# Cross-attention loop: half of the low softmax weights on GpSimd, one maximum a slot, key chunks of the pair after next begun early

## What is computed

```python
kv_rope = kv_c * cos + rotate_half(kv_c) * sin                 # 4096 x 128
q_r     = einsum('bshq,hqr->bhsr', q_big, W_qr)                # 16 heads, 256 x 64
k_r     = einsum('bld,hdr->bhlr', kv_rope, W_kr)               # 16 heads, 4096 x 64
scores  = einsum('bhsr,bhlr->bhsl', q_r, k_r)
attn    = softmax(scores, axis=-1)
ctx_c   = einsum('bhsl,bld->bhsd', attn, kv_rope)              # 16 heads, 256 x 128
```

## Time and profile before

| | us |
|---|---|
| median of 3 runs | 735.45 (735.08 to 735.92) |
| profiled execution | 732.78 |
| its span | 731.0 |
| loop over the pairs, first score to last low part | 84.25 to 501.44 |

### The profile page before, as it was taken

One profiled execution on the slowest core, in us unless ns is written; L12 is line 12 of the kernel. 1 busy time (PEld: TensorE's weight loads), 2 busy tenths in 40 slices (PEclk: granted clock), 3 DMA queues, 4 the chain that ended last, 5 costly groups with the idle time before them and its releaser, 6 DMA issues.

```text
span 731.0 us, 14846 instructions
## 1 busy us (share of the span) xinstructions
PE 643.4 (88%) x5860; PEld 454.7 (62%) x5860; DVE 446.8 (61%) x581; ACT 382.1 (52%) x564; POOL 48.8 (7%) x72
## 2 busy tenths in 40 slices
PE   5699899899899898898898898898978988899447
PEld 4666577676676676776676776796546875642112
DVE  2977688698698688688688688453134854300001
ACT  2543576676675676676675775783125863110000
POOL 2430000000000000000000000000001310000000
PEclk9999999999999999999999999999998997999868
DMA  9902795224224224224224224205983051289991
GB/s 359 419 35 44 148 356 109 50 46 92 49 43 91 48 43 91 48 43 91 48 43 91 48 47 88 49 2 199 420 345 145 1 186 74 87 345 421 418 416 67
DMA packets 25106, 105.04 MB, mean 144 GB/s; under 512 B 3696, under 2 KB 6896, under 8 KB 19184
## 3 DMA queue, kind: packets, MB, share of 16 engines
q1 hardware_dynamic: 25072, 104.57, 44.3%
HBM read 77.29 MB, written 0.52 MB: 106 GB/s over the span
## 4 chain that ended last, share of the span: by engine, by line
PE 61%; DVE 17%; issue 8%; ACT 6%; DMA 4%; SPq 3%; POOL 1%; DVEq 0%; ACTq 0%
PE psO L985 7%; PE psO L993 6%; DVE arena L693 6%; PE psO L986 5%; PE psS L973 5%; PE psS L972 5%; PE psM L945 5%; DVE arena L711 5%; PE psO L1057 4%; DMA arena<-w_exp 3%; SPq L360 3%; PE psS L1199 3%; PE psO L909 2%; PE psO L931 2%; PE psO L933 2%
## 5 line engine op out<-in xcount | busy, mean ns | idle before, releaser
L711 DVE TENSOR_TENSOR arena<-arena 128x1024 bf16<-128x1024 f32 x128 | 156.7, 1224 | 79.8 <-ACT arena L513 78.1
L511 ACT ACTIVATE arena<-psS 128x1024 bf16<-128x1024 f32 x128 | 131.2, 1025 | 113.2 <-PE psS L973 112.9
L693 DVE TENSOR_REDUCE arena<-psM 128x2 f32<-128x1024 f32 x128 | 155.9, 1218 | 14.8 <-PE psM L945 14.8
L985 PE MATMUL psO<-arena 128*128 128x129 bf16 x1024 | 133.4, 220 | 7.6 <-ACT arena L504 7.2
L986 PE MATMUL psO<-arena 128*128 128x128 bf16 x1024 | 132.5, 220 | 0.0
L513 ACT ACTIVATE arena<-psS 128x1024 f32<-128x1024 f32 x128 | 130.6, 1021 | 0.0
L972 PE MATMUL psS<-arena 128*128 128x256 bf16 x512 | 120.8, 273 | 0.8 <-ACT arena L497 0.8
L973 PE MATMUL psS<-arena 65*128 65x256 bf16 x512 | 120.8, 273 | 0.0
L985 PEld LDWEIGHTS psO<-arena 128*128 128x128 bf16 x1024 | 98.0, 98 | 30.3 <-issue 20.7
L986 PEld LDWEIGHTS psO<-arena 128*128 128x128 bf16 x1024 | 99.4, 97 | 0.4
L993 PE MATMUL psO<-arena 128*128 128x129 bf16 x1024 | 79.4, 220 | 8.8 <-DVE arena L711 8.4
(11 more groups left out here) (188 smaller groups left out, 738.9 us busy)
## 6 DMA issues: line engine op xcount, KB each, us to landing
arena<-w_exp SPq DMA_DIRECT2D x32, 1024.0 KB, 16.4
arena<-arena SPq DMA_DIRECT2D x96, 256.0 KB, 3.7
arena<-w_exp SPq DMA_DIRECT2D x32, 512.0 KB, 17.4
arena<-w_pair SPq DMA_DIRECT2D x8, 1088.0 KB, 16.9
arena<-w_o SPq DMA_DIRECT2D x1, 4096.0 KB, 20.4
arena<-ctx SPq DMA_DIRECT2D x4, 512.0 KB, 13.6
arena<-rope SPq DMA_DIRECT2D x4, 512.0 KB, 14.5
arena<-w_shared_in SPq DMA_DIRECT2D x1, 2048.0 KB, 8.3
```

The lines of the kernel that those rows point to most:

```text
L511: nc.scalar.activation(p_hi[:, s % 2, :], psS[s % 2][:, :], ACT.Exp).then_inc(s_phi, 1)
L693: nc.vector.reduce_max(maxes[:, :, st, c], psM[:, :].rearrange("p (j n) -> p j n", j=2), AX.X).then_inc(s_mfree, 1)
L711: nc.vector.tensor_tensor(p_lo[:, s % 2, :], p_f[:, s % 2, :], p_hi[:, s % 2, :], ALU.subtract).then_inc(s_plo, 1)
L985: mm(psC[:, st, :], ph, vx[:, GROUP * g + i, 0:CW], start=g == 0 and i == 0 and st == 0, stop=False, skip_group_check=True)
```

## The change

A plan, made once, says for each slot which key chunks and maxima of the next pair (1) and of the one after it (2) are done. Each engine now has four bodies: ENTRY for pair 0, STEADY for pairs 1 to 5, LAST_BUT_ONE, LAST.

```diff
+def plan(first, after):
+    keys = [(1, c, c if first else 2 * c - 4) for c in range(0 if first else 2, CHUNKS)]
+    keys += [(2, c, SLOTS - 4 + c) for c in range(2)] if after else []
+    at = [2, 3, 4, 4, 5, 6, 6, 7, 8, 8, 9, 10, 10, 11, 12, 13] if first else [None, None, *range(BIAS_SLOT)]
+    maxima = [(1, m, slot) for m, slot in enumerate(at) if slot is not None]
+    maxima += [(2, m, BIAS_SLOT + m) for m in range(2)] if after else []
+    return [[[(d, n) for d, n, slot in what if slot == s] for what in (keys, maxima)] for s in range(SLOTS)]
+BIAS_SLOT = SLOTS - 2
+ENTRY, STEADY, LAST_BUT_ONE, LAST = plan(True, True), plan(False, True), plan(False, False), [[[], []]] * SLOTS
```

SyncE, the order of the copies (each still with its two waits):

```diff
+                keys_of(0, 0)
+                queries_of(0)
+                keys_of(1, 0)
+                keys_of(0, 1)
+                keys_of(1, 1)
+                queries_of(1)
```

GpSimd does the low weights of even slots, and copies queries and key weights for the early chunks to places of their own (the first two pairs don't need them):

```diff
+            def bring_next(q):
+                if not (isinstance(q, int) and q == 2):
+                    wait_apart(pool, s_mmm, (q - 1) * MAXIMA + 2, pool_passed)
+                nc.gpsimd.tensor_copy(q_max_next, q1_all[:, bass.ds(q * 2, 2), :]).then_inc(next_copied, 1)
+                nc.gpsimd.tensor_copy(wkr_next[:, 0, :], wkr_hi[:, bass.ds(q * P, P)]).then_inc(next_copied, 1)
+                nc.gpsimd.tensor_copy(wkr_next[:, 1, :], wkr_lo[:, bass.ds(q * P, P)]).then_inc(next_copied, 1)
+            def low_part(p, s):
+                wait_apart(pool, s_pf, p * SLOTS + s + 1, pool_passed)
+                wait_apart(pool, s_pv, p * SLOTS + s - 1, pool_passed)
+                nc.gpsimd.tensor_tensor(p_lo[:, s % 2, :], p_f[:, s % 2, :], p_hi[:, s % 2, :], ALU.subtract).then_inc(s_plo[0], 1)
+            def body(p, after=True):
+                for s in range(0, SLOTS, 2):
+                    if s == 0 and not (isinstance(p, int) and p == 0):
+                        normalise(p * 2 - 1)
+                    if s == HALF:
+                        normalise(p * 2)
+                    low_part(p, s)
+                    if after and s == 4:
+                        bring_next(p + 2)
+                    if after and s == BIAS_SLOT - 2:
+                        bring(p + 2)
```

ScalarE gives `head_out` and `bias_rows` to VectorE, and casts a chunk in the chunk's own slot:

```diff
-                    wait(act, s_pv, t - 1)
+                    wait(act, s_hi, t - 1)
+                    wait(act, s_plo[s % 2], p * HALF + s // 2)
                     nc.scalar.activation(p_hi[:, s % 2, :], psS[s % 2][:, :], ACT.Exp).then_inc(s_phi, 1)
-                    wait(act, s_plo, t - 1)
                     nc.scalar.activation(p_f[:, s % 2, :], psS[s % 2][:, :], ACT.Exp).then_inc(s_pf, 1)
-                    if s == HALF:
-                        head_out(p, 0)
-                    if s == 0 and not (isinstance(p, int) and p == 0):
-                        head_out(p - 1, 1)
-                    if ahead and 1 <= s <= CHUNKS:
-                        keys_high(p + 1, s - 1)
-                    if ahead and s == BIAS_SLOT + 1:
-                        bias_rows(p + 1)
+                    for d, c in todo[s][0]:
+                        keys_high(p + d, c)
```

VectorE:

```diff
+            def bias_rows(q):
+                wait(dve, s_scores, q * SLOTS)
+                dve.wait_ge(s_tmm, q + 1)
+                nc.vector.tensor_copy(q2[R:R + 1, :, :], psO[1][R:R + 1, :].rearrange("p (j s) -> p j s", j=2)).then_inc(s_bias, 1)
+            def head_out(p, j):
                 hd = p * 2 + j
+                dve.wait_ge(s_pv, hd * HALF + HALF)
+                wait(dve, ctx_done, hd)
+                nc.vector.tensor_copy(raw, psC).then_inc(s_out, 1)
                 dve.wait_ge(s_out, hd + 1)
                 nc.vector.reciprocal(rsum, raw[:, :, K]).then_inc(s_rsum, 1)
...
+                    if s == 0 and not (isinstance(p, int) and p == 0):
+                        head_out(p - 1, 1)
+                    if s == HALF:
+                        head_out(p, 0)
+                    keys, maxima = todo[s]
+                    if s == BIAS_SLOT and todo is not LAST:
+                        bias_rows(p + 1)
+                    for d, m in maxima[0:1]:
+                        maximum(p + d, m)
+                    if s % 2:
+                        dve.wait_ge(s_pf, t + 1)
+                        wait(dve, s_pv, t - 1)
+                        nc.vector.tensor_tensor(p_lo[:, s % 2, :], p_f[:, s % 2, :], p_hi[:, s % 2, :], ALU.subtract).then_inc(s_plo[1], 1)
+                    for d, c in keys:
+                        keys_low(p + d, c)
+                    for d, m in maxima[1:2]:
+                        maximum(p + d, m)
```

TensorE multiplies the low part of a slot one slot later; the bias rows go to psO[1], so they wait for `s_kfree`:

```diff
                     if s < SLOTS - 1:
                         scores(p, s + 1)
-                    if now:
-                        maximum(p + 1, now[0])
+                    elif todo is not LAST:
+                        scores(p, SLOTS)
+                    if s % 2 == 0 and s:
+                        context_lo(p, s - 1)
+                    if s == 0 and not (isinstance(p, int) and p == 0):
+                        context_lo(p - 1, SLOTS - 1)
+                    if s == BIAS_SLOT and todo is not LAST:
+                        bias(p + 1, todo is not LAST_BUT_ONE)
+                    for d, m in maxima[0:1]:
+                        maximum(p + d, m)
+                    for d, c in key_steps:
+                        keys(p + d, c)
                     context_hi(p, s)
-                    if s == SLOTS - 1 and ahead:
-                        scores(p, SLOTS)
-                    if ahead and s < CHUNKS:
-                        keys(p + 1, s)
-                    context_lo(p, s)
-                    if now[1:]:
-                        maximum(p + 1, now[1])
-                    if ahead and s == BIAS_SLOT:
-                        bias(p + 1)
+                    for d, m in maxima[1:2]:
+                        maximum(p + d, m)
+                    if s % 2:
+                        context_lo(p, s - 1)
```

More of the change, by code:

```diff
@@ L429, in _ @@
             bring(1)
-            normalise(0)
-            with pool.Fori(2, NPAIR) as q:
-                bring(q)
-                normalise(q * 2 - 3)
-                normalise(q * 2 - 2)
-            for h in range(H - 3, H):
-                normalise(h)
+            def body(p, after=True):
[9 more added lines that the diff above has]
+                        bring(p + 2)
+            body(0)
+            with pool.Fori(1, NPAIR - 2) as p:
+                body(p)
+            body(NPAIR - 2, after=False)
+            body(NPAIR - 1, after=False)
+            normalise(H - 1)
             for h in range(NH2):
@@ L492, in keys_high, with body @@
                 nc.scalar.copy(k_hi[:, 512 * c:512 * c + 512], bank[:, :]).then_inc(s_khi, 1)
[L494 to L506 removed]
+            def body(p, todo):
                 for s in range(SLOTS):
@@ L526, in _ @@
                     keys_high(0, n)
-                elif what == "t":
-                    bias_rows(0)
-                elif what != "m" and (what != "hk" or rest[0] == DC - 1):
+                elif what not in "mt" and (what != "hk" or rest[0] == DC - 1):
                     query(what, n)
-            body(0)
-            with act.Fori(1, NPAIR - 1) as p:
-                body(p)
-            body(NPAIR - 1, ahead=False)
-            head_out(NPAIR - 1, 1)
+            body(0, ENTRY)
+            with act.Fori(1, NPAIR - 2) as p:
+                body(p, STEADY)
+            body(NPAIR - 2, LAST_BUT_ONE)
+            body(NPAIR - 1, LAST)
             for h in range(H):
@@ L712, in body @@
                     if s == HALF:
-                        one_over_sum(p, 0)
-                    if s == 0 and not (isinstance(p, int) and p == 0):
-                        one_over_sum(p - 1, 1)
-                    if ahead and 1 <= s <= CHUNKS:
-                        keys_low(p + 1, s - 1)
-                    if ahead:
-                        for m in maxima_in(s):
-                            maximum(p + 1, m)
+                        head_out(p, 0)
+                    keys, maxima = todo[s]
@@ L733, in _ @@
                     maximum(0, n)
-            body(0)
-            with dve.Fori(1, NPAIR - 1) as p:
-                body(p)
-            body(NPAIR - 1, ahead=False)
-            one_over_sum(NPAIR - 1, 1)
+                elif what == "t":
+                    bias_rows(0)
+            body(0, ENTRY)
+            with dve.Fori(1, NPAIR - 2) as p:
+                body(p, STEADY)
+            body(NPAIR - 2, LAST_BUT_ONE)
+            body(NPAIR - 1, LAST)
+            head_out(NPAIR - 1, 1)
             for h in range(H):
```

103 lines of the change are left out of this document (50 added, 53 removed).

## The result

| | before | after |
|---|---|---|
| median of 4 runs each, us | 735.68 (735.08 to 738.35) | 715.49 (713.25 to 717.88) |
| profiled execution, its span | 732.78, 731.0 | 717.11, 715.2 |
| first score to last low part | 84.25 to 501.44: 417.2 | 85.29 to 480.95: 395.7 |
| behind the loop, to the span's end | 229.6 | 234.3 |

The ratio is 0.9721, 95% interval 0.9683 to 0.976: 20.2 us less by the medians. The forecast was 710.5 with a range of 699 to 727, so the time lies inside it and 5 us above the forecast.

A forecast was written before the change was run, and what follows sets the result against it. Bound: TensorE, alternating with VectorE in slots 10 to 13 and a TensorE-ScalarE-TensorE hand-over. Of 39.8 us waiting 13.4 remain; gain 26.4, less 1.4 kept back, is 25: 732.78 to 707.8, median 710.5, range 699 to 727.

The forecast's parts named there:

- five middle pairs: Loop pairs 1 to 5: remaining TensorE waiting of 1.2 us at odd slots plus 0.3 at slot 14 each, 7.5 together.
- last pair: Last head pair: 2 x 0.55 us waiting for the uncovered psC copies plus 0.3 for the last low part, 1.4.
- kept back: 1.4 us taken off the summed gain of 26.4 for hand-overs not seen, leaving 25.
- I take 0.17 at seven odd slots: TensorE's low part waits for VectorE's odd subtraction: 0.17 us, between 0.11 and 0.24, at seven odd slots, 1.2 a pair.
- TensorE reaches the maximum at T+0.89: Odd slot, T being its score start: the maximum begins 0.89 us later, putting the odd subtraction's end at T+3.65.
- the first bias copy comes about 0.4 later, under the load of ScalarE's table: Before the loop: the bias copy's delay of about 0.4 us was to be hidden, with no cost.
- GpSimd's pass: GpSimd's 128x1024 subtraction in even slots, taken as 2.2 us with ends 2.0 and 4.3; free up to 3.9.
- rival A: GpSimd becomes the loop's bound through a ring with ScalarE; at 4.3 us a pass, pair 55.2, total 760; 7%.
- Rival B: In-order chains cost more: odd low parts wait 0.35 to 0.5 us, bias slot 0.6 to 1.0; total 719 to 728; 18%.
- C: Casts of early key chunks wait for the copies, 2 to 3 us in each of six pairs; total 725; 6%.
- D: Nearly all the loop's waiting goes: gain 33 to 37 us, total 700; 14%.
- 0.9 us that was priced: VectorE's two-SBUF-input passes and GpSimd's passes lengthening each other: price 0, at most 0.9 us where they meet.

The follow-up runs named there:

- experiment 2: Changed kernel with the old spread of maxima and key chunks, no work for the pair after next, GpSimd's subtractions kept; 737.95 us, ratio 1.0017.
- experiment 7: Changed kernel with the psC copy back on ScalarE behind the exponentials of slots 8 and 0, late low part kept; 714.2 us, ratio 0.972.
- experiment 4: Changed kernel with the key and query copies issued in the old order; 752.46 us, ratio 1.0202.
- experiment 1: Changed kernel with the low parts of even slots moved from GpSimd back to VectorE; 724.86 us, ratio 0.9833.
- experiment 10: Changed kernel run once more without an edit; 714.46 us, ratio 0.9726, 234.1 us behind the loop.
- experiments 1 to 9: Follow-up kernels, each the changed kernel with one or more further edits; measured from 707.53 to 765.04 us.
- experiment 3: Changed kernel with GpSimd's subtraction done twice, first into a spare place; 765.04 us, ratio 1.0383.
- experiment 6: Changed kernel with VectorE subtracting before reducing in odd slots of pairs 1 to 6, except slots 13 and 15; 707.53 us, ratio 0.9641.

## Why the prediction was right, and where its sum was off

**The mechanism.** The two places named as the source of the waiting were the right ones: the pairs of maxima in slots 10 to 13 (experiment 2: without the plan these slots stay at 15.1 us) and the hand-over over psC (gone, by experiment 7 through the order). The plan could take the early chunks only with the new order of copies (experiment 4). GpSimd's part, which the sum did not price by itself, is worth 9.4 us (experiment 1).

**The sum.** The loop's 377.4 us of TensorE work and the terms of remaining waiting, as predicted and as the trace after shows them:

| term | predicted | after |
|---|---|---|
| five middle pairs | 7.5 (5 x 1.5) | 9.75 (5 x 1.95) |
| pair 6 | 1.5 | 2.6 (50.0 between marks; its start is shared with the last pair) |
| pair 0 | 3.0 | 3.2 |
| last pair | 1.4 | 2.7 |
| kept back | 1.4 | none |
| start of the loop | 0 | 1.04 |
| together | 14.8 | 19.3 |

The difference is 4.5; the predicted gain of 25 less 4.5 is 20.5, and the medians differ by 20.2. In the profiled execution alone the gain is 15.7, because it also has the 4.7 us behind the loop of experiment 10.

**The terms that were mis-sized.** First the odd low part, "I take 0.17 at seven odd slots", bounds 0.11 and 0.24. It is 0.25, the upper bound. The step that was off is the first one of the chain, "TensorE reaches the maximum at T+0.89". TensorE's starts in one pair of slots after:

```profile
295.39 0.27 PE L1018 MATMUL psS<-arena 128*128 128x256 bf16 x1
...
296.37 0.39 PE L989 MATMUL psM<-arena 64*128 64x512 bf16 x2
```

The maximum starts at T+0.98, the reduction at T+1.41 (296.80) where 1.29 was taken, the subtraction (297.94) ends at T+3.77 instead of T+3.65, and the low part starts at T+3.83 (299.22) where TensorE wanted it at T+3.59. The whole chain is 0.12 later, and the wait is 0.24 in place of 0.11 without anything else being lost. Seven times 0.25 is 1.75 of the 1.95 in a middle pair; 0.2 is left for slot 14 against the 0.3 taken. Second the last pair: psC's two waits are 0.61 each against the predicted 0.55, but behind its mark the low part of slot 13 of pair 6 waits another 0.51 for its subtraction, which VectorE does behind the last reduction and the negative maxima, and the last low part waits 0.50 against the predicted 0.3. TensorE's and VectorE's timelines after:

```profile
436.52 0.18 DVE L714 TENSOR_REDUCE arena<-arena 128x4 f32<-128x32 f32 x1
...
436.82 1.22 DVE L748 TENSOR_TENSOR arena<-arena 128x1024 bf16<-128x1024 f32 x1
...
438.10 0.63 PE L1040 MATMUL psO<-arena 128*128 128x129 bf16 x8 [0.51 <-DVE arena L748]
...
444.38 0.22 PE L1031 MATMUL psO<-arena 128*128 128x129 bf16 x1 [0.61 <-ACT arena L538]
```

(The second wait names ScalarE, whose exponential was written long before; VectorE's copy of psC runs from 443.81 to 444.24 and is what came last.) Pair 6 is short of this plan's key work but not of its waits; its share was set equal to a middle pair's without being worked out.

Third the start. The step that failed is "the first bias copy comes about 0.4 later, under the load of ScalarE's table": its size is about right, but the table load does not cover it. First the kernel before, from its first negative maxima, then the kernel after:

```profile
82.53 0.18 DVE L696 TENSOR_REDUCE arena<-arena 128x4 f32<-128x32 f32 x1
...
83.53 0.58 ACT L497 CAST arena<-psM 1x512 bf16<-1x512 f32 x1
```

```profile
83.00 0.18 DVE L714 TENSOR_REDUCE arena<-arena 128x4 f32<-128x32 f32 x1
...
84.00 1.28 ACT L538 ACT_TABLE_LOAD   x1
84.01 0.42 DVE L640 TENSOR_TENSOR arena<-psS,arena 64x256 bf16<-64x256 f32 x1
...
84.46 0.69 DVE L722 CAST arena<-psO 1x512 bf16<-1x512 f32 x1
...
85.29 0.27 PE L1018 MATMUL psS<-arena 128*128 128x256 bf16 x1 [1.41 <-DVE arena L722]
...
86.38 1.02 ACT L538 ACTIVATE arena<-psS 128x1024 bf16<-128x1024 f32 x1 [1.10 <-PE psS L1019]
```

On VectorE the copy is queued behind a subtraction for the queries and takes 0.69 instead of 0.58, so from the negative maxima to the first score it is 2.29 us instead of 1.72. Before, the first exponential (85.42) came right behind the table load (84.12 to 85.40); after, the load ends at 85.28 and the exponential waits for the scores until 86.38. That is 0.57 of the 1.04 us. The other 0.47 were there before the first bias copy: the negative maxima come at 83.00 instead of 82.53. They can't come from the moved copy, and nothing shows that they come from the change: in the kernels of experiments 1 to 9, which have the same program up to there, they come between 82.38 and 83.91.

**The rest.** GpSimd's pass was the largest unknown, 2.0 to 4.3, and the line through the undisturbed rows (2.2 against 2.13) was right. So rival A did not come; experiment 3 shows that its price for a middle pair was right. Half of the 4497 ns that the Trainium skill ("GPSIMD Engine Reference", 3.1) gives for 2048 columns, 2.25 us, an estimate, is 6% above the trace. Rival B named the mechanism that is left, at a larger size than it has. C needs the old order. D did not come either; experiment 6 goes towards it, 27.4 us below its kernel before against D's 33 to 37, with middle pairs within 1.1 us of what TensorE needs.

## What to carry to other kernels

Price a serial hand-over by what the freed buffer makes the other engine wait (here 0.49 us a maximum on a single psM), because taking work off the engine that reduces gave nothing in slots 10 to 13 (experiment 2). In an in-order queue ask of each pair of neighbours whose consumer comes first; swapping two neighbours took another 5.7 us out of the loop. And when work is begun earlier, the copies that free its target must be reordered with it, or one queue entry that waits takes the whole gain and more, the fall of the granted clock behind the wait included.

## What was not expected of the hardware

VectorE and GpSimd hold each other up more than the 0.9 us that was priced, and more than the 1.2 that the prediction worked out from the rule. In the last pair of the kernel after:

```profile
445.08 2.13 POOL L440 TENSOR_TENSOR arena<-arena 128x1024 bf16<-128x1024 f32 x1
445.32 2.98 DVE L748 TENSOR_TENSOR arena<-arena 128x1024 bf16<-128x1024 f32 x1 [0.88 <-ACT arena L539]
```

The subtraction, issued 0.24 later, ends 1.09 after GpSimd's, 2.98 long instead of 1.22. At 436.82 it was the other way: VectorE's was first and took 1.22, GpSimd's took 3.09. Whoever comes second starts when the first has ended; the Trainium skill ("SBUF — State Buffer", Who interferes with whom) says so, and the trace agrees, to within 0.13 us in both cases. So the price is the rest of the other's pass (1.76 us at 445) and not one pass of its own. TensorE shows no wait for the subtraction at 445, so it cost nothing there. A tiny operation can pay the whole price: in experiment 2 a negation of 4 columns, with a single tensor input, came 0.49 after the start of GpSimd's subtraction and took 1.66 us instead of 0.17. TensorE's bias rows waited 1.88 for it. The same comes back in each of pairs 0 to 5. (The same section counts tensor_scalar among the operations that can take the shared ports, and the trace agrees.) VectorE's and GpSimd's timeline of that kernel:

```profile
240.67 2.12 POOL L441 TENSOR_TENSOR arena<-arena 128x1024 bf16<-128x1024 f32 x1
...
241.16 1.66 DVE L715 TENSOR_SCALAR arena<-arena 128x4 bf16<-128x4 f32 x1
```

And the granted clock falls where work is alike. In the first 15 us behind the loop it was 0.89 or 1.00; the profiles with 0.89 there are 3.5 to 4.1 us longer behind the loop (234.3 and 234.1 against 230.6 and 230.2). Whoever compares two profiles has to take that out first: of the 9.5 us between those of experiment 6 and the kernel after, 3.7 are not in the loop.
